# Local attention rebuilt as a pipeline of 64-query units, and new ends of two cross-attention layers, in a two-layer Perceiver kernel

## What is computed

```python
x = x + L0_xattn(LN(x), ctx)      # 8 heads of 64
x = x + L0_attn(LN(x))            # window attention + pooled latents (below)
x = x + L0_ffn(LN(x))             # 8 experts, top 2
x = x + L1_xattn(LN(x), ctx)      # 16 heads of 16
x = x + L1_attn(LN(x))            # RWKV-like scan
x = x + L1_ffn(LN(x))             # 8 experts, top 2
```

```python
# every block of 64 queries sees its own 64 keys and the 64 before them,
# causal and within a distance of 64; the first block sees only its own
local  = softmax(mask(Qb @ Kw.T / 4)) @ Vw
# x @ wgk and x @ wgv are averaged over groups of 4 tokens: 64 latents
remote = softmax(lmask(GQ @ GK.T / 4)) @ GV            # 8 heads
gl, gr = sigmoid(sum(Q * gate_local_w)), sigmoid(sum(Q * gate_remote_w))  # per head
out    = (gl * local + gr * (remote @ r_out_w)) @ w_out
```

## Time and profile before

| | |
|---|---|
| runs | 1763.49, 1770.37, 1771.4 us; median 1770.37 |
| profiled execution | 1762.66 us; span of its trace 1760.9 us |
| granted TensorE clock, mean | 0.924 |
| busy: TensorE, VectorE, ScalarE, GpSimd | 88%, 61%, 42%, 28% of the span |
| local attention stage | 586.80 to 756.60 us of the span |

### The profile page before, as it was taken

The page is one execution under the profiler, slowest core; times in us unless marked ns, Lnnn a source line. Parts: engine busy times, 40 slices in busy tenths (PEclk is TensorE's granted clock), DMA queues, the critical chain, the costliest instruction groups (busy, mean ns, idle before and its releaser), DMA issues. The chain is left out here.

```text
span 1760.9 us, 25971 instructions
## 1 busy us (share of the span) xinstructions
PE 1544.8 (88%) x9943; PEld 1151.1 (65%) x9943; DVE 1070.6 (61%) x1687; ACT 737.3 (42%) x990; POOL 500.8 (28%) x630
## 2 busy tenths in 40 slices
PE   7979999999999668879998787998999899974298
PEld 6768887877877467768997564455665454442288
DVE  5856666666642464466665798877766775016641
ACT  4535555544544132234442113554555455842120
POOL 1005524435569000000000202544444544820000
PEclk9999999999999876779998998999999999986599
DMA  4333334323322200022222122211111110000263
GB/s 167 144 96 108 121 110 130 132 82 99 109 63 46 61 1 1 0 88 81 95 96 71 72 96 72 73 72 49 49 72 73 49 48 1 1 16 10 96 199 99
DMA packets 68528, 134.25 MB, mean 76 GB/s; under 512 B 8722, under 2 KB 38980, under 8 KB 68420
## 3 DMA queue, kind: packets, MB, share of 16 engines
q1 hardware_dynamic: 68228, 132.74, 23.0%
q10 hardware_dynamic: 192, 0.05, 0.0%
HBM read 98.64 MB, written 17.30 MB: 66 GB/s over the span
## 5 line engine op out<-in xcount | busy, mean ns | idle before, releaser
L860 ACT ACTIVATE P<-score 128x1024 f32<-128x1024 f32 x256 | 255.5, 1023 | 173.7 <-PE score L1274 173.7
L651 POOL CAST st<-ef 32x512 fp32r<-32x512 f32 x384 | 233.7, 609 | 318.6 <-PE score L1274 274.4
L1859 DVE TENSOR_REDUCE mx<-bank 128x1 f32<-128x512 f32 x384 | 247.4, 686 | 103.8 <-PE bank L1289 102.4
L1274 PE MATMUL score<-qs,st 97*128 97x512 f32 x512 | 176.7, 437 | 5.1 <-DMA qs<-shift 4.3
L1749 DVE TENSOR_REDUCE mx<-bank 128x1 f32<-128x512 f32 x192 | 123.7, 686 | 73.7 <-PE bank L1113 65.0
L616 POOL TENSOR_TENSOR sum<-sum,P 128x512 f32<-128x512 f32 x84 | 111.5, 1327 | 182.9 <-ACT P L774 182.9
L1289 PE MATMUL bank<-ef,qm 128*128 128x512 f32 x384 | 142.5, 433 | 19.2 <-DVE mx L1859 14.3
L774 ACT ACTIVATE P<-score 128x1024 f32<-128x1024 f32 x128 | 129.4, 1024 | 67.3 <-PE score L1099 64.9
L1063 PE MATMUL bank<-w_split,c_hi 128*128 128x256 f32 x768 | 145.9, 290 | 0.6 <-ACT v L870 0.6
L1303 PE MATMUL bank<-P,v 128*17 128x256 f32 x2048 | 137.0, 388 | 0.0
L1274 PEld LDWEIGHTS score<-qs,st 97*128 97x128 f32 x512 | 86.1, 194 | 75.1 <-ACT P L860 34.2
(11 more groups left out here) (333 smaller groups left out, 2748.5 us busy)
## 6 DMA issues: line engine op xcount, KB each, us to landing
c_hi<-split_ctx SPq DMA_DIRECT2D x48, 512.0 KB, 3.3
c_lo<-split_ctx SPq DMA_DIRECT2D x48, 512.0 KB, 4.3
w<-k SPq DMA_DIRECT2D x128, 128.0 KB, 3.5
arena<-in_L_ffn_W SPq DMA_DIRECT2D x16, 1024.0 KB, 5.2
c_in<-in_ctx SPq DMA_DIRECT2D x16, 512.0 KB, 3.9
split_ctx<-c_hi SPq DMA_DIRECT2D x16, 512.0 KB, 3.6
split_ctx<-c_lo SPq DMA_DIRECT2D x16, 512.0 KB, 4.8
w1raw<-in_L_ffn_w SPq DMA_DIRECT2D x8, 1024.0 KB, 4.9
```

The lines of the kernel that those rows point to most:

```text
L651: pool.tensor_copy(st1[32 * block:32 * block + 32, k, :], ef1[rows, g % ERING, part, :].bitcast(F32)).then_inc(a[f"st{k}"], 16)
L860: act.activation(P1[:, index % PRING, :], score[n % 2][:], ACT.Exp).then_inc(a["p"], 1)
L1274: last = mm(score[n % 2][:, 512 * j:512 * j + 512], st1[0:97, pair, 128 * k:128 * k + 128], qs1[0:97, u % 2, 2 * pair:2 * pair + 2, :], st ...
L1859: v.tensor_reduce(mx1[:, u % 2, i, n:n + 1], bank_of(a, g + 1, f"m{n}")[:], AX.X, ALU.max).then_inc(a["red"], 1)
```

## The change

Local attention becomes ten units in one pipeline: eight windows of 64 queries with all 16 heads, and two latent units (one for each sequence, all its 256 queries), in the order latent 0, window 0, window 1, latent 1, windows 2 to 7. The masked copies of the queries are made once, in advance, for all blocks: four masks of eight by VectorE, one by ScalarE, three by GpSimd. A pair of heads shares one product: their masked queries of 64 make the 128 weight columns. Scores have three buffers in on-chip memory. All evictions of turned weights go to ScalarE. The scale of the scores moves into the masks. The gates are computed for 64 queries at a time with both halves of the partitions. The weights are loaded by SP at step 32 of layer 0's cross-attention, w_out in 16 pieces. Each engine's new order:

```diff
+        LA_UNITS = [("latent", 0), ("window", 0), ("window", 1), ("latent", 1), *(("window", n) for n in range(2, BLOCKS))]
@@ SP, cross0
                     if t == CHUNKS:
                         sp.wait_ge(a["vp"], a.n("vp", 2 * CHUNKS))
                         sp.dma_start(wout0[:], ...)
+                        attention_weights()
+                for r in range(2):
+                    for a in range(PAIRS):
+                        sp.dma_start(la_wout[HD * a:HD * a + HD, r], rows[r, a]).then_inc(la["w"], 16)
@@ GpSimd, local_attention
+                for f in range(2):
+                    pool.wait_ge(la["pa"], 3 * f + 1)
+                    for l in range(1, 4):
+                        last = pool.tensor_scalar(la_Qm[:, 4 * f + l // 2, :, l % 2, :], la_QT[:, f, :]..., la_maskq[:, l:l + 1], None, ALU.mult)
@@ ScalarE, local_attention
+                for n in range(2):
+                    act.wait_ge(la["pv"], 3 + n)
+                    act.activation(la_V[:, 4 + 2 * n:6 + 2 * n, :, 0:HD], bank[2 + n]..., ACT.Copy).then_inc(la["pa"], 1)
+                def exponentials(n):
+                    act.wait_ge(la["m"], n + 1)
+                    if LA_UNITS[n][0] == "latent":
+                        act.activation(la_S[:, n % 3], la_S[:, n % 3], ACT.Exp).then_inc(la["e"], 1)
+                        return
+                    for k in range(PAIRS):
+                        part = la_S[:, n % 3, 128 * k:128 * k + 128]
+                        last = act.activation(part, part, ACT.Exp, bias=la_m[:, n % 3, k:k + 1])
+                    last.then_inc(la["e"], 1)
+                exponentials(0)
+                for n in range(len(LA_UNITS)):
+                    if n + 1 < len(LA_UNITS):
+                        exponentials(n + 1)
+                    if n >= 2:
+                        act.wait_ge(la["o"], n - 1)
+                    for k in range(2):
+                        act.wait_ge(la["tr"], 2 * n + k + 1)
+                        act.activation(la_PT[:, n % 2, 512 * k:512 * k + 512], bank[2 + k][:], ACT.Copy).then_inc(la["pt"], 1)
+                    if n:
+                        turned_context(n - 1)
@@ TensorE, local_attention
+                def scores(n):
+                    kind, k = LA_UNITS[n]
+                    dst = score[n % 2]
+                    if n >= 2:
+                        pe.wait_ge(la["sb"], n - 1)
+                    if kind == "latent":
+                        for u in range(2):
+                            last = mm(dst[:, 512 * u:512 * u + 512], la_GQT[...], la_GK[:, k]..., start=True, stop=True)
+                    else:
+                        for a in range(PAIRS):
+                            last = mm(dst[:, 128 * a:128 * a + 128], la_Qm[:, a, k]...,
+                                      la_KT[:, a // 4, WIN * k:WIN * k + 128], start=True, stop=True)
+                def gates():
+                    for n in range(BLOCKS):
+                        for r in range(2):
+                            for f in range(2):
+                                last = mm(bank[3][64 * r:64 * r + 64, 384 + 16 * n:400 + 16 * n], la_QT[:, f, WIN * n:WIN * n + WIN],
+                                          la_G[:, f, r]..., tile_position=(0, 64 * r))
+                scores(0)
+                gates()
+                pe.wait_ge(la["msk"], 3)
+                scores(1)
+                values(2)
+                values(3)
+                for n in range(len(LA_UNITS)):
+                    if n + 2 < len(LA_UNITS):
+                        scores(n + 2)
+                    turn(n)
+                    if n:
+                        combined(n - 1)
+                    attend(n)
+                    if n:
+                        output(n - 1)
+                combined(len(LA_UNITS) - 1)
+                output(len(LA_UNITS) - 1)
@@ VectorE, local_attention
+                masked_scores(0)
+                window_values(0)
+                window_values(1)
+                masked_scores(1)
+                dve.wait_ge(la["ga"], 1)
+                for n in range(len(LA_UNITS)):
+                    if n:
+                        combine(n - 1)
+                    if n > 1:
+                        residual_sum(n - 2)
+                    if n + 2 < len(LA_UNITS):
+                        masked_scores(n + 2)
+                    if n:
+                        gated_remote(n - 1)
```

```diff
@@ TensorE, output
-                for n in range(TT):
-                    if n == 0:
-                        pe.wait_ge(a["o"], a.n("o", 2))
-                    if n == 2:
-                        sums(UNITS - 1)
-                        pe.wait_ge(a["o"], a.n("o", 4))
...
+                pe.wait_ge(a["o"], a.n("o", 3))
+                bias_row(0)
+                for k in range(2):
+                    heads(0, k)
+                sums(UNITS - 1)
...
+                for n in range(2, 4):
+                    bias_row(n)
+                    for k in range(2):
+                        heads(n, k)
+                for k in range(2, 4):
+                    pe.wait_ge(a["o"], a.n("o", 2 + k))
+                    for n in range(2, 4):
+                        last = heads(n, k)
@@ VectorE
+            def divide_last(a, n, oT, den, sums):
+                v.reciprocal(den[:, n, :], sums[:, S * n:S * n + S]).then_inc(a["rd"], 1)
+                return v.tensor_tensor(out, out, den[:, n, :], ALU.mult)
@@ GpSimd, cross0
-                    for h in range(3):
+                    for h in range(3 if g + 1 < CHUNKS else 1):
```

```diff
@@ TensorE, cross1
                     if t == 0:
+                        pe.wait_ge(set1["wTc"], 1)
+                        queries(0)
                         pe.wait_ge(set1["whl"], 2)
                     if t == 1:
-                        queries()
-                        output_weights()
-                        pe.wait_ge(set1["q"], 2)
-                        pe.wait_ge(set1["wop"], 2)
+                        pe.wait_ge(set1["q"], 1)
...
+                            if h == 6 and 1 <= t <= 3:
+                                queries(t)
+                            if h == 6 and t in (4, 5):
+                                output_weights(t - 4)
```

More of the change, by code:

```diff
@@ L309, in perceiver @@
[L309 to L322 removed]
+              "w msk xp pj pa pd gt gp ga pv s sb m e tr pt o cb ct ctc rem rg out res".split()}
@@ L1401, in local_attention @@
             def local_attention():
-                pe.wait_ge(la["w"], 192)
-                step = [0]
-                def project(pairs, out=None):
-                    n = step[0]
-                    if n >= 2:
-                        pe.wait_ge(la["pe"], n - 1)
-                    dst = bank[2 + n % 2][:] if out is None else out
-                    width = pairs[0][1].free_size()
-                    for k, (l, r) in enumerate(pairs):
-                        last = mm(bank[2 + n % 2][:, 0:width], l, r, start=(k == 0), stop=(k == len(pairs) - 1))
-                    last.then_inc(la["pj"], 1)
-                    step[0] += 1
@@ new lines, in turn @@
+                def turn(n):
+                    pe.wait_ge(la["e"], n + 1)
+                    for k in range(2):
+                        if n:
+                            pe.wait_ge(la["pt"], 2 * n - 1 + k)
+                        else:
+                            pe.wait_ge(la["pa"], 8 + k)
+                        for j in range(4):
+                            last = nc.tensor.transpose(bank[2 + k][:, 128 * j:128 * j + 128],
+                                                       la_S[:, n % 3, 512 * k + 128 * j:512 * k + 128 * j + 128], ident[:])
+                        last.then_inc(la["tr"], 1)
@@ new lines, in output @@
+                def output(n):
+                    kind, k = LA_UNITS[n]
+                    if kind == "latent" or k % 2 == 0:
+                        return
+                    pe.wait_ge(la["ctc"], k + 1)
+                    for r in range(2):
+                        last = mm(bank[1][:, 256:512], la_cT[:, k // 2 % 2, r, :], la_wout[:, r, :], start=(r == 0), stop=(r == 1))
+                    last.then_inc(la["out"], 1)
+                for f in range(2):
+                    for w in range(2):
+                        project(score[f][:, TOK * w:TOK * w + TOK], [(la_wqkv[:, w, k, 128 * f:128 * f + 128], xnT[:, k, :]) for k in range(2)]).then_inc(la["pj"], 1)
@@ new lines, in local_attention @@
+                masked_queries(1)
+                dve.wait_ge(la["pj"], 6)
+                for b in range(B):
+                    v.tensor_tensor(la_GK[:, b], bc(bank[3][:, LAT * b:LAT * b + LAT], 1, NHG), bc(la_maskq[:], 2, LAT), ALU.mult).then_inc(la["pd"], 1)
+                for b in range(B):
+                    for r in range(2):
+                        rows = slice(64 * r, 64 * r + 64)
+                        last = v.tensor_copy(la_GV[rows, b, :, HD * r:HD * r + HD],
```

(19 more changed lines are left out.)

569 lines of the change are left out of this document (303 added, 266 removed).

## The result

The changed kernel takes 1669.7 us (median, 1664.7 to 1673.2) against 1766.9 in the same measurement, a ratio of 0.945 (0.943 to 0.948): 5.5% faster. The forecast was 1702, with 1682 as the lower end of its range. The direction was right and the gain was half as large again as forecast: 97 us, not 65. The profiled execution took 1667.4 (span 1665.3), 95.3 less than that of before.

What follows compares the result with a forecast made beforehand. No engine was full in the old local attention; TensorE would pace the new units. Savings 38.1 + 6.2 + 8.9 + 11.4 = 64.6 took 1762.7 to 1698; allowing for the median's shift, 1702 us, range 1682 to 1742.

Steps and rivals of the forecast that it cites:

- the end of layer 0: End of layer 0's cross-attention: additions moved to VectorE and a halved reciprocal save 6.7 us, 6.2 net of SP's queue.
- the beginning of layer 1: Start of layer 1's cross-attention: first maxima come about 10.2 us earlier; less 1.3 given back later, 8.9 us less.
- its end: End of layer 1's cross-attention: earlier products of ones, halved reciprocal and no low clock; 11.4 us less.
- Transposes 2 x 1.04 = 2.1: Local attention pipeline: a window unit's 8 transposes on TensorE are 16 records and take 2.1 us.
- The gates ... I take 9: Start of the local attention: the gates' 64 narrow records on TensorE take 9 us, bounds 7.7 and 15.4.
- Scores of window 0 at the low clock 3.6: Start of the local attention, behind the gates: window 0's score products run at the low clock and take 3.6 us.
- 13 us: Local attention pipeline: loss to clock falls in about four of nine units, the last two mostly low.
- GpSimd's sums lag ... and use the pause, so I count 0.5.: Layer 0: weight DMAs delay TensorE 2.6 us, but GpSimd's lagging sums absorb most; 0.5 us lost, bounds 0 and 2.6.
- 1.3: Layer 1 after its first maxima: VectorE's work for the other three query blocks gives back 1.3 us of the gain.
- the clock low throughout: Rival for the local attention pipeline: clock stays low, stage 174 us, total 1740 (1736 to 1745); chance 0.16.
- the clock that never falls: Rival for the local attention pipeline: narrow stretch too short to lower the clock; 1685, shifted 1689 us; chance 0.18.
- the serial case: Rival for the local attention: units don't overlap, 19.2 us each, stage 233, total 1800 us; chance 0.05.

Runs made afterwards that it cites:

- both doublings: Two runs against the changed kernel: each value product of a window unit issued twice, 1687.8 us; VectorE's maximum of each window unit taken twice, 1669.2 us.

## Why the prediction was right or wrong

**Right.** The stage's bound (TensorE's order, both doublings); layer norm and drain; where it puts the clock's falls, in kind (in a middle unit and in the last two); the end of layer 0 (6.1 us for 6.7, before the queue); the beginning of layer 1 (first maxima 15.75 us after its start, 16.1 forecast); its end (10.2 for 11.4, each step some tenths longer). GpSimd's six masked copies took 10.55 us, within 4 to 15, and cost nothing.

**Wrong, by size.**
1. "Transposes 2 x 1.04 = 2.1" (pipeline). The row of 8 records of 1.04 us was read as one bank; a bank takes four transposes, and the 8 are two banks, the whole unit. The prediction's own sentence "16 records each" was false for transposes, and its "up to 36" for the old code counted them one record each. It cost 1.2 us a unit, 11 us over the nine. The value products at 1.81, the cheap latent unit (1.0 for its values) and the sum itself (its terms add up to 7.1, not 7.2) are the rest: the nine units are 47.6 at the high clock, where 61.7 stood.
2. "The gates ... I take 9" (bounds 7.7 and 15.4). Measured 2.06. The bounds were taken from rows with 128 weight columns. They allowed neither for narrower products (0.053 a record within one half) nor for two halves that work at once (0.032).
3. "Scores of window 0 at the low clock 3.6": 2.05, since the gates were too short to lower it. With 1 and 2 this makes the first unit's end 9.6 us earlier (6.9 + 1.6 + 1.1); the other terms of that part cancel.
4. "13 us" for the clock in the pipeline. The slow groups of records cost 0.7 + 1.6 (scores), 0.8 + 0.9 (transposes), 1.65 (values), 0.9 (output) and 0.2 (turned context), together 6.7 us. The forecast had falls in about four of the nine units and the last two low; the trace has one in the middle, the tail of one at the beginning, and the last two.
5. "GpSimd's sums lag ... and use the pause, so I count 0.5." TensorE lost 1.9 us (2.6 forecast, 1.7 to 4.5 over the profiles), and all of it stood in the layer's end. GpSimd's last addition ended 74.0 us after the load of the output weights (569.2 - 495.2); the same addition of before, the fifth from its end, 71.8 after it (565.3 - 493.6). So it was as late as TensorE, and no pause was absorbed. This went against the gain and was small.
6. The "1.3" that layer 1 should give back was not seen: from its first maxima to its last value products it took 575.1 for 578.4. As that stage took 600.2 to 605.7 us in profiles of the same code, this difference is open.

The sum of 1 to 4 is 9.6 + 14.1 + 6.3 = 30 us, the stage's whole miss. The rivals: the clock low throughout was refuted (0.86 on average over the nine units, 0.98 in the first half of them); the clock that never falls came nearest with 1689, but not by its mechanism, since the clock did fall, and of the 32 us from 1702 to the 1670 measured 18 are transposes and gates; the serial case was shown to exist with the lead cut by one.

## What to carry to other kernels

Count the records of a row against the loops of the code before its duration is used as a unit price: one row may span two banks, and a transpose is one record where a product is two. For an operation with no row, the lower bound has to allow for the best packing of the array, not only for the nearest row. When one engine's idle wait is moved and the time stays, look at the order on the engine that is waited for: here a reordering that did not shorten its stage alone made it 8 us shorter together with one on the other engine. And take a stage's idle and busy time apart before it is called unchanged: 2.2 us of added idle time stood against 2.6 us less of busy time, at a higher clock.

## What the runs showed of the hardware

- A record of an fp32 product of 64 weight columns and 16 columns took 0.032 us when the products alternate between the halves of TensorE and 0.053 in one half; of 128 weight columns and 34 columns 0.11 (1.81 for 16; all at clock 1.00). An fp32 transpose of 128x128 is one record of 0.13 us (8 in 1.04).
- With one unit's lead TensorE was idle 48.7 us in the stage (16.5 with two), and the granted clock was 0.69 (0.85). The same records took it 28 us longer, so the lower clock cost nearly as much as the 32 us of added idle time.
- The same code of layer 0, up to the load of its output weights, took from 490.7 to 497.9 us in the profiles here, layer 1's cross-attention from 600.2 to 605.7, the local attention of one code from 101.7 to 104.3. A smaller difference of a whole stage says nothing without a fixed point inside it.
- A DMA issue took SP 0.5 us also for pieces of 16 rows (8.38 for 16).
